# Graph attention layer on one Trainium2 core: alternating Q and K halves, scores six steps ahead, attention two steps ahead, first projections as group -1

## What is computed

```python
q = heads(x @ Wq + bq); k = heads(x @ Wk + bk); v = heads(x @ Wv + bv)
scores = einsum('bhqd,bhkd->bhqk', q, k) / sqrt(32)
scores = where(adj == 0, -inf, scores)
attn = softmax(scores, axis=-1)
out = einsum('bhqk,bhkd->bhqd', attn, v).reshape(b, s, 512)
y = layernorm(x + out @ Wo + bo)
```

## Time and profile before

| what | value |
|---|---|
| median of 3 runs | 904.38 us |
| profiled execution, device time | 906.47 us |
| profiled execution, span | 904.7 us |
| TensorE busy | 870.5 us (96%) |
| VectorE busy | 810.5 us (90%) |
| ScalarE busy | 689.5 us (76%) |
| GpSimd busy | 272.3 us (30%) |
| chain that ended last, TensorE's share | 93% |

### The profile page before, as it was taken

One profiled execution on the slowest core, in us unless ns is written; L12 is line 12 of the kernel. 1 busy time (PEld: TensorE's weight loads), 2 busy tenths in 40 slices (PEclk: granted clock), 3 DMA queues, 4 the chain that ended last, 5 costly groups with the idle time before them and its releaser, 6 DMA issues.

```text
span 904.7 us, 32198 instructions
## 1 busy us (share of the span) xinstructions
PE 870.5 (96%) x11784; PEld 607.9 (67%) x11784; DVE 810.5 (90%) x3449; ACT 689.5 (76%) x1745; POOL 272.3 (30%) x386
## 2 busy tenths in 40 slices
PE   6989999999999999999999999999999999999954
PEld 4666667776667777666777666777766677766632
DVE  5779999999999999999999999999999999999983
ACT  5777778877788877787887778877778788777761
POOL 0113233332233332323333223333232333322222
PEclk9999999999999999999999999999999999999967
DMA  8267899879789988799887779898889998778773
GB/s 302 59 129 123 161 182 183 164 152 153 151 171 179 177 169 153 136 167 182 181 159 172 144 148 169 178 177 161 145 159 159 182 178 171 156 141 158 149 135 93
DMA packets 362414, 144.98 MB, mean 160 GB/s; under 512 B 340752, under 2 KB 344848, under 8 KB 361872
## 3 DMA queue, kind: packets, MB, share of 16 engines
q1 hardware_dynamic: 362256, 142.93, 81.6%
HBM read 42.21 MB, written 16.78 MB: 65 GB/s over the span
## 4 chain that ended last, share of the span: by engine, by line
PE 93%; DVE 4%; DMA 1%; issue 1%; ACT 0%; SPq 0%; POOL 0%; POOLq 0%; DVEq 0%
PE proj_ps L605 76%; PE score_ps L605 9%; PE av_ps L605 8%; DVE masked L492 1%; DVE p_pair L479 1%; DMA w_land<-weights 1%; DVE y L518 0%; DMA aT<-a_pair 0%; DVE stats L521 0%; DVE v_parts L465 0%; DVE a_pair L458 0%; ACT probs L407 0%; ACT p_pair L417 0%; SPq L253 0%; DVE inv_sum L501 0%
## 5 line engine op out<-in xcount | busy, mean ns | idle before, releaser
L407 ACT ACTIVATE probs<-masked,minus_max 128x128 f32<-128x128 f32 x1024 | 327.0, 390 | 167.2 <-DVE minus_max L492 166.3
L492 DVE CUSTOM_DVE_ANT_0 masked<-score_ps,mask 128x128 f32<-128x128 f32 x1024 | 237.4, 287 | 45.1 <-PE score_ps L605 39.8
L479 DVE SCALAR_TENSOR_TENSOR p_pair<-probs,p_pair 128x512 f16<-128x512 f32 x256 | 197.6, 772 | 1.3 <-ACT p_pair L417 1.0
L605 PE MATMUL proj_ps<-wo_hi,aT 128*128 128x512 f16 x512 | 166.3, 387 | 2.7 <-DMA aT<-a_pair 1.6
L417 ACT ACTIVATE p_pair<-probs 128x512 f16<-128x512 f32 x256 | 161.3, 630 | 8.1
L225 POOL TENSOR_TENSOR xT_lo<-xT_raw,xT_hi 128x512 f16<-128x512 f32 x60 | 69.9, 1165 | 317.0 <-ACT xT_hi L370 317.0
L605 PE MATMUL proj_ps<-xT_hi,wq_hi 128*128 128x256 f16 x512 | 141.7, 277 | 8.6 <-DVE wq_lo L573 7.6
L605 PE MATMUL proj_ps<-xT_lo,wq_hi 128*128 128x256 f16 x512 | 141.2, 276 | 0.0
L605 PE MATMUL proj_ps<-xT_hi,wq_lo 128*128 128x256 f16 x512 | 141.2, 276 | 0.0
L605 PE MATMUL proj_ps<-xT_hi,wk_hi 128*128 128x256 f16 x512 | 140.2, 274 | 0.0
L605 PE MATMUL proj_ps<-xT_hi,wk_lo 128*128 128x256 f16 x512 | 139.6, 273 | 0.0
(11 more groups left out here) (58 smaller groups left out, 1521.2 us busy)
## 6 DMA issues: line engine op xcount, KB each, us to landing
xT_raw<-x_cols SPq DMA_DIRECT2D x32, 512.0 KB, 4.5
x_in<-x_rows SPq DMA_DIRECT2D x32, 512.0 KB, 5.4
out<-y SPq DMA_DIRECT2D x64, 256.0 KB, 4.6
adj_in<-adj SPq DMA_DIRECT2D x32, 128.0 KB, 2.9
pT<-p_pair SPq DMA_TRANSPOSE x256, 3.4
w_land<-weights SPq DMA_DIRECT2D x2, 1024.0 KB, 7.5
w_land<-weights SPq DMA_DIRECT2D x4, 256.0 KB, 4.8
x_res<-weights SPq DMA_DIRECT2D x1, 1024.0 KB, 9.3
```

Source lines behind the costliest of these rows:

```text
L407: ins = act.activation(probs[s % 2][:, j * S:(j + 1) * S], masked[s % 2][:, j], ACT.Exp, bias=minus_max[s % 2][:, j:j + 1], scale=-1.0)
L479: dve.scalar_tensor_tensor(out=p_pair[s % NT][:, HW:2 * HW], in0=probs[s % 2][:], scalar=P_UP, in1=p_pair[s % NT][:, 0:HW], op0=ALU.mult, ...
L492: ins = dve.tensor_tensor_reduce(masked[s % 2][:, j], score_ps[j][:, s % HC], mask[par][:, s // KC], -EXP_SCALE, 3.0e38, ALU.add, ALU.min, ...
L605: return pe.matmul(dst, lhsT, rhs, start=first, stop=last)
```

## The change

- `TASKS` becomes Q0, K0, Q1, K1, V0, V1, Y1, Y0. Step 6 makes Y1 of group g-1, step 7 makes Y0 of group g itself. `RANK` follows the order of `TASKS`.
- The attention is moved against the projections. In step s of group g the unit numbers are now s+6 for `scores`, s+5 for the maximum and the exponentials, s+4 for the low part and the turning of the probabilities, s+2 for `attend` and s+1 for `head_norm` (`at_work`). All of these were at s+1, s, s-1, s-3 and s-4; the distances between them stay. So units 0 to 5 of group g+1 are scored in steps 2 to 7 of group g, while that group's banks are made.
- `scores` of unit 0 now waits for K0 and that of unit 2 for K1, each made in the step before (`split_no(g, K, c // 2)`).
- VectorE's list: `y_and_moments` in steps 7 and 0, `low_part_attn` in steps 1 and 3, `make_mask` in step 2. ScalarE's: `high_part_attn` in steps 0 and 3, `high_part_x` in steps 2 and 4. GpSimd's: `normalize` in steps 0 and 1, `residual` in 2 and 4 as before, `low_part_x` in 3 and 5. SyncE's order follows.
- The prologue becomes a group -1 that runs the same steps; the low parts of Wv and Wo are made within it and within group 0, b_out goes through a projection bank in its step 6, and group 0's first bank waits for it.
- The increments of `vector_goes`, `gpsimd_goes` and `sync_goes` are removed.

```diff
-    TASKS = ((Q, 0), (Q, 1), (K, 0), (K, 1), (V, 0), (Y, 0), (V, 1), (Y, 1))
-    LAG = 3
+    TASKS = ((Q, 0), (K, 0), (Q, 1), (K, 1), (V, 0), (V, 1), (Y, 1), (Y, 0))
+    SCORED, MAXED, TURNED, ATTENDED, NORMED = 6, 5, 4, 2, 1
+    RANK = {t: n for n, t in enumerate(TASKS[:6])}
...
+    def at_work(g, s, ahead):
+        u = unit(g, s) + ahead
+        return [divmod(u, SLOTS)] if 0 <= u < NG * SLOTS else []
...
             def normalize(g, b):
                 pool.wait_ge(moments_done, n + 1)
-                pool.sem_inc(gpsimd_goes, 1)
...
                 pool.wait_ge(ln_small, n * 3 + 3)
-                pool.sem_inc(gpsimd_goes, 1)
...
         @block.gpsimd
+            def group(g, par):
                 for s in range(SLOTS):
+                    if s == 0 and g >= 2:
+                        normalize(g - 2, 1)
+                    if s == 1 and g >= 1 and has_next(g):
+                        normalize(g - 1, 0)
+                    if s == (2 if has_next(g) else 0) and g >= 0:
+                        residual(g, 0, par)
+                    if s == (4 if has_next(g) else 0) and g >= 0:
+                        residual(g, 1, par)
+                    if s in (3, 5) and has_x_next2(g):
+                        low_part_x(pool, g + 2, (s - 3) // 2, par)
...
         @block.scalar
+            def group(g, par):
+                    if s == 0 and g >= 1:
+                        high_part_attn(g - 1, 1)
+                    if s == 3 and g >= 0:
+                        high_part_attn(g, 0)
+                    if 1 <= s <= N_SPLIT and has_next(g):
+                        high_part_bank(g + 1, *TASKS[s - 1], nxt)
+                    if g == -1 and s == 2:
+                        high_part_weight("v")
+                    for unit_g, t in at_work(g, s, MAXED):
+                        exponentials(unit_g, t)
+                        high_part_probs(unit_g, t)
+                    if s in (2, 4) and has_x_next2(g):
+                        high_part_x(g + 2, (s - 2) // 2, par)
...
         @block.vector
+            def group(g, par):
+                    for unit_g, t in at_work(g, s, MAXED):
+                        masked_max(unit_g, t, unit_g % 2)
+                    for unit_g, t in at_work(g, s, TURNED):
+                        low_part_probs(unit_g, t)
+                    if 1 <= s <= N_SPLIT and has_next(g):
+                        low_part_bank(g + 1, *TASKS[s - 1], nxt)
+                    if s == 1 and g >= 1:
+                        low_part_attn(g - 1, 1)
+                    if s == 3 and g >= 0:
+                        low_part_attn(g, 0)
+                    for unit_g, t in at_work(g, s, NORMED):
+                        head_norm(unit_g, t)
+                    if g == -1 and s == 2:
+                        low_part_weight("v", range(KC))
+                    if s == 2 and has_next(g):
+                        make_mask(g + 1, nxt)
...
+                    if s == (0 if has_next(g) else 3) and g >= 1:
+                        y_and_moments(g - 1, 0, nxt)
+                    if s == SLOTS - 1 and g >= 1 and has_next(g):
+                        y_and_moments(g - 1, 1, nxt)
+                    if s == 5 and not has_next(g):
+                        y_and_moments(g - 1, 1, nxt)
...
             def scores(g, s, par):
-                if s == 0:
-                    pe.wait_ge(split_out, split_no(g, K, 1) + 1)
+                if b == 0 and c % 2 == 0:
+                    pe.wait_ge(split_out, split_no(g, K, c // 2) + 1)
...
         @block.tensor
+            def group(g, par):
+                    if has_next(g):
+                        step_bank(g, s, par)
+                        for unit_g, t in at_work(g, s, ATTENDED):
+                            attend(unit_g, t, unit_g % 2)
+                        for unit_g, t in at_work(g, s, SCORED):
+                            scores(unit_g, t, unit_g % 2)
+                        continue
...
+            for g in range(-1, NG):
+                group(g, g % 2)
```

More of the change, by code:

```diff
@@ L61, in split_no, with bank_of @@
         return g * N_SPLIT + RANK[kind, i]
-    def bank_of(kind, i, prologue=False):
-        if prologue:
-            return RANK[kind, i] % NB
+    def bank_of(kind, i):
         return TASKS.index((kind, i)) % NB
-    def y_bank_of(g, b):
-        return b if isinstance(g, int) and g == LAST else bank_of(Y, b)
     def x_half_no(g, h):
@@ L88, in wait @@
     def wait(eng, sem, value):
-        if not isinstance(value, int) or value > 0:
+        if value > 0:
             eng.wait_ge(sem, value)
-    def at_least(g, n):
-        return not isinstance(g, int) or g >= n
     def has_next(g):
-        return not isinstance(g, int) or g < LAST
+        return g < LAST
     def has_x_next2(g):
[L100 to L111, removed]
+        return g < LAST - 1
+    def at_work(g, s, ahead):
+        u = unit(g, s) + ahead
+        return [divmod(u, SLOTS)] if 0 <= u < NG * SLOTS else []
     with ExitStack() as ctx:
@@ L280, in group @@
                         load_xT(g + 2)
-                    if s == 1 and at_least(g, 1):
+                    if g == -1 and s == 1:
+                        sp.wait_ge(w_lo_made, KC)
+                        load_w("o")
+                        sp.dma_start(b_out[:], bo.partition_broadcast(P)).then_inc(bo_loaded, 16)
+                    if g == -1 and s in (5, 6):
+                        load_x(s - 5, s - 5)
+                    if s == 1 and g >= 1:
+                        turn_attn(g - 1, 1)
                         if has_next(g):
@@ L295, in _ @@
             load_w("v")
[L296 to L305, removed]
+            for g in range(-1, NG):
+                group(g, g % 2)
             store(LAST - 1, 0)
-            turn_attn(LAST, 0)
+            turn_attn(LAST, 1)
             store(LAST - 1, 1)
-            turn_attn(LAST, 1)
             for b in range(GB):
@@ L356, in _ @@
             pool.wait_ge(const_made, 2)
[L357 to L360, removed]
+            for g in range(-1, NG):
+                group(g, g % 2)
+            for b in range(GB):
+                normalize(LAST - 1, b)
+            for b in range(GB):
+                normalize(LAST, b)
         @block.scalar
@@ L673, in step_bank, with b_out_bank @@
                     pe.wait_ge(split_out, split_no(g + 1, *TASKS[s - 2]) + 1)
-                elif not at_least(g, 1):
-                    pe.wait_ge(split_out, split_no(g, V, s) + 1)
-                elif s == 0:
-                    pe.wait_ge(split_out, split_no(g, V, 1) + 1)
-                elif at_least(g, 2):
-                    pe.wait_ge(y_summed, batch(g - 2, 1) + 1)
-                else:
-                    pe.wait_ge(split_out, split_no(g, K, 1) + 1)
-                split_bank(g + 1, kind, i, nxt)
+                elif s == 0 and g >= 2:
+                    pe.wait_ge(y_summed, batch(g - 2, 1) + 1)
+                elif s == 0 and g == 1:
+                    pe.wait_ge(split_out, split_no(g, V, 0) + 1)
+                elif s == 0 and g == 0:
+                    pe.wait_ge(b_out_made, 1)
+                elif s == 1 and g >= 1:
+                    pe.wait_ge(y_summed, batch(g - 1, 0) + 1)
+                elif s == 1 and g == 0:
+                    pe.wait_ge(split_out, split_no(g, V, 1) + 1)
+                split_bank(g + 1, kind, i, nxt, g == -1 and i == 0)
+            def b_out_bank():
+                pe.wait_ge(w_loaded["o"][0], 16)
+                pe.wait_ge(bias_made, 2)
+                for ki in range(KC):
+                    ins = mm(b_out_ps[:], b_v_wide[:, ki], w_raw["o"][:, ki], ki == 0, ki == KC - 1)
+                ins.then_inc(b_out_mm, 1)
             def scores(g, s, par):
```

254 lines of the change are left out of this document (83 added, 171 removed).

## The result

The changed kernel takes 933.07 us (median of 4 runs, 932.26 to 933.77) against 904.49 us, a ratio of 1.0316 (95% interval 1.0292 to 1.0339): slower by 3.2%. The forecast was 937 with a range of 904 to 950. The profiled execution spans 931.8 us.

The account below looks back on a forecast made before the run. TensorE bounds the steady middle, so the change wins only at the ends: 904.7 + 4.9 (beginning) - 14.9 (end) + 42.6 (middle waits) = 937.3, adjusted by 1.77 and 2.09 to 937 us; range 904 to 950.

Parts of the forecast that it names:

- K0, 0.9 a group: Step 2: scores of unit 0 wait for K0's late split; TensorE loses 0.77 to 1.27 us a group, taken as 0.9.
- the increments, which I had bounded at 0.25 on VectorE: Removed semaphore increments give back 0 to 0.25 us on each engine, working against the K0 wait.
- The collision, 1.12: Step 1: GpSimd's `residual` starts first and holds up VectorE's `low_part_attn`, which ends at 4.07, not 2.95: 1.12 us lost.
- The tie of 0.04 us: Step 1: GpSimd's `residual` was forecast to start only 0.04 us ahead of VectorE's `low_part_attn`.
- rival 1: Middle: only K1 waits, 6 to 20 us in all; time 901 to 915, middle 908; chance 0.18.
- K1, 0.52 a group: Step 4: scores of unit 2 wait for K1's split; TensorE loses 0.52 us a group, 0.2 without the second collision.
- step 3's own collisions: Step 3: low parts meet GpSimd's `low_part_x` and `residual`, losing 0.68 and 0.31 us; the step takes 3.25 + 0.99.
- The beginning, +4.9: Before group 1: group 0 takes 25.5 us, group 1 begins at 61.5, 4.9 us later; bounds 2 to 8.
- The end, -14.9: Last group: ends 31.2 us after its start instead of 46.12, 14.9 sooner; bounds 12 to 18.
- only the ends count: Rival 2: nothing waits in the middle; 894 us, between 889 and 900; chance 0.12.
- A falling clock in the middle: Rival 3: pauses lower TensorE's clock; one half-speed bank costs 2.6 us a group, above 1000; chance 0.08 with rival 4.
- feed each other past 1.8: Rival 4: middle waits feed each other and pass 1.8 us a group, above 949; chance 0.08 with rival 3.

Follow-up runs that it names:

- `x_res` earlier: Changed kernel with GpSimd making the first x_res of a group in step 0, after the first layer norm, not step 2: 907.76 us, 1.0032.
- the idle instruction: Changed kernel plus one idle GpSimd instruction on a 128x1 tile ahead of the first x_res of each group: 908.52 us, 1.0035.
- the runs with SyncE's list: Changed kernel with both x_res moved (steps 0 and 6), plus SyncE's x_in load and second-batch store moved from step 1 to 4: 899.72 us, 0.995.
- the low parts in steps 3 and 4: Changed kernel with both x_res moved, plus a_pair's low parts and their turning in steps 3 and 4, not 1 and 3: 899.05 us, 0.9944.
- the repaired kernels: Changed kernel with both x_res moved, plus SyncE's transfers moved (899.72 us) or a_pair's low parts in steps 3 and 4 (899.05; with b_out's product later, 898.38).
- the low parts in steps 3 and 5: Changed kernel with VectorE's low parts of a_pair, and SyncE's turning of them, in steps 3 and 5, not 1 and 3: 933.63 us, 1.0327.
- the two repaired by moving transfers: Changed kernel with both x_res moved, plus SyncE's load and store in step 4 (899.72 us), or a_pair's low parts and turning in steps 3 and 4 (899.05).

## Why the prediction was right, and where its terms were off

**What bounds and where the change can lose.** Right. TensorE's middle was full, and most of what was lost was lost there: 34.8 us in 30 groups, against 42.6 forecast. The other 8.8 were lost at the beginning, which the forecast had at 4.9. The stretch without waits (757.00 busy of 757.00) shows that the base of 26.7 us a group holds.

**K0, 0.9 a group: 0.64.** The mechanism is as the prediction put it; the term was mis-sized through the increments, which I had bounded at 0.25 on VectorE. They are worth 0.62 in the path to step 2, and 1.27 - 0.62 = 0.65. A maximum that waits for scores starts 0.12 after TensorE's step, not 0.30, and a step with Y takes 3.44, not 3.66:

```profile
480.89 0.39 PE L571 MATMUL proj_ps<-wo_hi,aT 128*128 128x512 f16 x1
```
```profile
481.01 0.29 DVE L468 CUSTOM_DVE_ANT_0 masked<-score_ps,mask 128x128 f32<-128x128 f32 x1 [0.77 <-PE score_ps L571]
...
484.33 0.18 DVE L501 BATCH_NORM_AGGREGATE moments<-stats 128x2 f32<-128x6 f32 x1
484.45 0.29 DVE L468 CUSTOM_DVE_ANT_0 masked<-score_ps,mask 128x128 f32<-128x128 f32 x1
```

With these, VectorE begins step 2 at 0.12 + 3.44 + 3.44 + 3.25 = 10.25 after step 7 began, plus 1.05 of collision. The split is done 2.32 later, at 13.62, where TensorE wants it at 13.04. The difference, 0.58, and 0.06 from the split's end to the scores are the 0.64. Without the collision VectorE would begin step 2 at 10.25, 0.10 late, and its split would be done at 12.57, ahead of TensorE. Then nothing waits, and that is what two runs show (`x_res` earlier, and the idle instruction).

**The collision, 1.12: 1.05.** Right in place and size. The tie of 0.04 us on which rival 1 hung was 0.09 in the changed kernel. I had argued with the increments on both engines; that `x_res` would be first came true, but not as argued. With VectorE's increments put back the lead is 0.09 to 0.10 as well, since the layer norm ahead of `x_res` is itself held by the low part of `p_pair` and ends 0.64 us after it. So the order did not hang on luck from group to group. But the prediction had not seen what fixes it, and that it fell on the right side of a tie of 0.04 us was luck. How thin it is the run with the idle instruction shows. Its time, 908.5, lies in rival 1's range (901 to 915), but nearly two thirds of its waits are attention's for turned probabilities, which rival 1 did not have.

**K1, 0.52 a group: 0.45.** The size is right, the account of it not quite. I had made it from step 3's own collisions. But when the collision in step 1 was taken away, K1's wait fell from 13.6 to 3.2 us. The larger part of it was step 1's lateness, handed on: step 3 began 0.53 after TensorE's step (467.56 against 467.03) and not 0.12. The forecast let step 3 begin 0.30 after TensorE's step, whatever had gone before, so it had no such term. Of the 0.53, 0.25 come from the mask at the end of step 2, which takes 0.59 us with the wait behind it and not the estimated 0.34; no run shows what this share costs TensorE. Against that, step 3's own collisions cost 0.43 + 0.29 = 0.72 us, not 0.99. That the two errors nearly cancel is luck.

**The wait for turned probabilities** (2.7 us) was not in the sum. I wrote that none of the attention's waits change, since their distances stay. What changed is who stands beside them in SyncE's list: a load and a store next to a turning, all in step 1, as the runs with SyncE's list and with the low parts in steps 3 and 4 show.

**The beginning, +4.9: +8.8.** Group 0's first bank came at 36.30, as forecast (36.0). Then group 0 took 29.1 us instead of 25.5. Two banks after pauses ran at the low clock (granted 0.62), 4.45 us each instead of 2.73, together 3.4, and the forecast had no term for them:

```profile
36.30 4.45 PE proj_ps L571 x24
...
60.37 4.45 PE proj_ps L571 x12
```

What put them at the low clock is not settled. In the run with the low parts in steps 3 and 4 the same Y bank, after a pause of the same size, took 2.76 us at clock 1.00.

**The end, -14.9: -16.4.** Right within its bounds of 12 to 18: 29.71 us for 31.2. The last Y bank ran at the full clock, 2.76 us, where the old kernel took 8.28 for two.

**Sum.** Middle 7.8 us less than forecast (836.7 against 844.5), beginning 3.9 more, end 1.5 less: 5.4 us, the difference between 937.3 and 931.8. The errors partly cancel (K0 alone was 7.7 us too high, the beginning 3.9 too low, and 2.7 us of waits were missing), so that 937 came so near to 933 is in part luck.

**Rivals.** That only the ends count (894, between 889 and 900) is what the repaired kernels come to, 898 to 900. A falling clock in the middle did not occur in the changed kernel: it is 1.00 with TensorE busy 96% there. The mechanism is real, as five groups of the run with the low parts in steps 3 and 5 show, but a slow bank costs 1.6 us more there and not the 2.6 that the rival put on it. The waits come to 1.19 us a group and did not feed each other past 1.8.

## What to carry to other kernels

When one engine is full, shifting work against it is judged by the other engines' lists, step by step: sum each step, carry the lateness forward, and compare it with the distance to the reader. Two loaded steps side by side and a shorter distance cost nothing by themselves here; with a collision of 1.05 us on top, the waits for K grew by 29 us. And a wait that ends at a DMA depends on what stands beside it in the queue, so moving a transfer is a change of the path too.

## What the runs showed of the hardware that I had not expected

- An increment of a semaphore between VectorE's instructions costs 0.2 us in a chain of short dependent ones (3.66 against 3.44 us for a step with Y) and 0.18 behind a wait (0.30 against 0.12). In a middle where VectorE has slack it costs next to nothing (26.73 us a group with, 26.71 without).
- Which of two instructions that exclude each other goes first was settled by starts 0.06 to 0.09 us apart, and came out the same way in every group: 1.72 or 1.73 us for all of the low parts of `a_pair` in step 1 of the changed kernel, 0.68 for all of them with the idle instruction. Such a near tie can be steady because an earlier collision sets it: GpSimd's layer norm ended 0.64 us after VectorE's low part of `p_pair`, whether it took 0.82 or 1.18 us itself.
- In a steady middle with a pause of TensorE of 1.7 to 2.5 us in eight groups, the next bank ran at the low clock in five of them (4.3 to 4.4 us instead of 2.70) and at the full one in three.
- Kernels in which attention waits 5.8 to 7.7 us for turned probabilities spread over 902 to 911 us from run to run; the two repaired by moving transfers, without that wait, over 897 to 902.
